# Gated cross-attention with two expert layers: the last stage's hidden layer computed transposed, its router weights spread over all partitions

## What is computed

```python
scores = jax.nn.sigmoid(x @ Wr)
_, idx = lax.top_k(scores + router_bias, TOP_K)              # 2 of 8 experts for each token
w = jnp.take_along_axis(scores, idx, axis=-1)
w = w / (jnp.sum(w, axis=-1, keepdims=True) + 1e-09)
cw = jnp.zeros((T, E), dtype=x.dtype).at[jnp.arange(T)[:, None], idx].add(w)
g = jnp.einsum('th,ehi->tei', x, Wg)                         # 4 networks, 256 -> 128
u = jnp.einsum('th,ehi->tei', x, Wu)
hid = jax.nn.silu(g) * u
mlp_out = jnp.einsum('tei,eih->teh', hid, Wd)                # 128 -> 256
routed = jnp.einsum('te,teh->th', cw[:, :E_MLP], mlp_out)
...
return routed + SHARED_SCALE * shared                        # shared: convolution over 4 tokens
```

## Time and profile before

| | before |
|---|---|
| median of 3 runs | 2226.85 us (2221.72 to 2227.82) |
| span of the profiled execution | 2225.1 us |
| PE busy | 2186.7 us, 98% |
| DVE busy | 1728.1 us, 78% |
| ACT busy | 1282.0 us, 58% |
| POOL busy | 645.1 us, 29% |
| last stage | from 1600.8 us to the end |

### The profile page before, as it was taken

One profiled execution on the slowest core, in us unless ns is written; L12 is line 12 of the kernel. 1 busy time (PEld: TensorE's weight loads), 2 busy tenths in 40 slices (PEclk: granted clock), 3 DMA queues, 4 the chain that ended last, 5 costly groups with the idle time before them and its releaser, 6 DMA issues. The chain is left out here.

```text
span 2225.1 us, 48355 instructions
## 1 busy us (share of the span) xinstructions
PE 2186.7 (98%) x15486; PEld 1865.5 (84%) x15486; DVE 1728.1 (78%) x6112; ACT 1282.0 (58%) x3251; POOL 645.1 (29%) x1162
## 2 busy tenths in 40 slices
PE   8999999999999999999999999999999999999997
PEld 6777777777777777777699999999878888888886
DVE  6788888888888888888675555555579999999986
ACT  6776776776776776776443333433345555555553
POOL 1123223222232232232220000000355555555541
PEclk9999999999999999999899999999999999999999
DMA  5320110110110110110052222221212222222210
GB/s 189 124 97 22 37 40 23 37 39 21 40 38 20 39 39 20 40 32 27 11 161 73 81 86 72 81 77 41 89 58 65 65 65 64 65 65 65 65 39 20
DMA packets 111642, 129.57 MB, mean 58 GB/s; under 512 B 14898, under 2 KB 98089, under 8 KB 111264
## 3 DMA queue, kind: packets, MB, share of 16 engines
q1 hardware_dynamic: 98249, 105.06, 14.9%
q0 software_dynamic: 12288, 21.21, 3.3%
q10 hardware_dynamic: 855, 0.19, 0.0%
HBM read 84.26 MB, written 54.53 MB: 62 GB/s over the span
## 5 line engine op out<-in xcount | busy, mean ns | idle before, releaser
L711 ACT ACTIVATE a_prob<-a_prob,a_nmax 128x376 f32<-128x376 f32 x512 | 309.7, 606 | 155.3 <-DVE a_nmax L857 155.3
L1457 ACT ACTIVATE e_hidden<-e_first,keep_b 128x256 f32<-128x256 f32 x320 | 134.1, 471 | 283.3 <-PE e_first L80 282.8
L857 DVE CUSTOM_DVE_ANT_0 a_prob<-a_score,a_mask_row 128x376 f32<-128x376 f32 x512 | 266.6, 540 | 10.8 <-issue 5.6
L80 PE MATMUL e_second<-e_w,e_hidden 128*128 128x256 f32 x1920 | 239.5, 284 | 0.0
L80 PEld LDWEIGHTS e_second<-e_w,e_hidden 128*128 128x128 f32 x1920 | 232.6, 192 | 0.0
L869 DVE TENSOR_SCALAR a_prob<-a_prob,a_rden 128x376 f32<-128x376 f32 x512 | 220.9, 453 | 2.5
L1151 PE MATMUL a_turned<-keep_ident,a_prob 128*128 128x128 f32 (+1 forms) x1536 | 217.3, 277 | 2.8 <-DVE a_probT L876 1.6
L1151 PEld LDWEIGHTS a_turned<-keep_ident,a_prob 128*128 128x128 f32 (+1 forms) x1536 | 173.5, 142 | 43.5 <-issue 27.6
L1142 PE MATMUL a_score<-a_kT,a_qT 64*128 64x376 f32 x1024 | 196.4, 502 | 0.0
L876 DVE COPY a_probT<-a_turned 128x384 f32<-128x384 f32 x256 | 139.8, 546 | 54.4 <-PE a_turned L1151 54.4
L719 ACT ACTIVATE a_probT<-a_turned 128x384 f32<-128x384 f32 x256 | 124.9, 488 | 92.1 <-PE a_turned L1151 91.7
(11 more groups left out here) (237 smaller groups left out, 5231.1 us busy)
## 6 DMA issues: line engine op xcount, KB each, us to landing
w_in<-W SPq DMA_DIRECT2D x32, 512.0 KB, 4.1
slots<-a_zeros SPq DMA_DIRECT2D x8, 1280.0 KB, 8.7
keep_rows<-slots SPq DMA_DIRECT2D x40, 256.0 KB, 3.9
answers<-e_y SPq DMA_DIRECT2D x40, 256.0 KB, 2.2
a_xn<-x SPq DMA_DIRECT2D x32, 256.0 KB, 2.9
a_xr<-x SPq DMA_DIRECT2D x32, 256.0 KB, 3.8
x<-r_x SPq DMA_DIRECT2D x32, 256.0 KB, 4.0
w_in<-x SPq DMA_DIRECT2D x32, 256.0 KB, 2.6
```

Of the source, the lines that this page charges most:

```text
L80: last = nc.tensor.matmul(out, stationary(a, t), moving(b, t), start=start and n == 0, stop=stop and n == len(todo) - 1)
L711: nc.scalar.activation(prob[:, u % 4, a], prob[:, u % 4, a], ACT.Exp, bias=nmax[:, u % 4, a:a + 1], scale=-1.0, accum_out=den[:, u % 4, a: ...
L857: nc.vector.tensor_tensor_reduce(prob[:, u % 4, a], score[SCORE_AT[u][a]][:, 0:NKV], mask_row[:, p], -1.0, 3.0e38, ALU.add, ALU.min, nmax[ ...
L1457: nc.scalar.activation(hidden[:, 2 * j + i], first[:, j, i * CH:(i + 1) * CH], ACT.Relu, bias=b1[:, 2 * j + i, bass.ds(e, 1)]).then_inc(re ...
```

## The change

- **Gate and up.** The weights of one network are now stationary and `x4T`, all 256 tokens of it, is moving: 12 matmuls of 256 columns for each pair `j` of networks, in place of 6 of 512 for each half of the tokens. The result has the hidden index on partitions and tokens along the row, for networks `2j` and `2j + 1`. `turn_hid` is gone.
- **Router weights.** A token's weight is now needed along the row, the same on all partitions. `cw` lies in a tile `cwp` padded to 32 columns. DVE transposes it in blocks of 32 (`weights_turned`), and SP writes the eight rows that matter, from each of the four blocks of partitions, to a DRAM tensor `chosen`, waits until they have landed, and reads all 4 KB of it back into every partition, into `cw_wide` (`spread_weights`).
- **The multiply** by these weights is done by POOL, on `hs`, in `share_hidden`, once for each pair. DVE then multiplies by `ups` in one instruction for each pair (`hidden`).
- **High and low parts** are made from `hid` in SBUF instead of from PSUM (`hidden_high` on ACT, `hidden_low` on DVE).
- **Down** sums by pairs of networks over both halves of the tokens, and both calls of `add_rest` are one. `down(s - 4, 0)` is at the end of PE's step now.

```diff
+            def spread_weights(b):
+                eng.wait_ge(cw_turned, b + 1)
+                for g in range(0, P, 32):
+                    eng.dma_start(t["chosen"][:, g:g + 32], cw_rows[g:g + EM * QT]).then_inc(cw_out, 16)
+                eng.wait_ge(cw_out, 16 * 4 * (b + 1))
+                at_least(eng, share_ok[1], b)
+                eng.dma_start(cw_wide[:].rearrange("p e s -> p (e s)"),
+                              t["chosen"].rearrange("c q -> (c q)").partition_broadcast(P)).then_inc(cw_in, 16)
...
             def step(s, p):
+                if live(s - 4):
+                    spread_weights(s - 4)
                 if live(s + 1):
                     early["load_x1"](eng, s + 1, 1 - p)
...
+            def share_hidden(b, j):
+                eng.wait_ge(hs_ok[j], b + 1)
+                eng.wait_ge(cw_in, 16 * (b + 1))
+                nc.gpsimd.tensor_tensor(hs[:, j].rearrange("p (e s) -> p e s", e=2),
+                                        hs[:, j].rearrange("p (e s) -> p e s", e=2), cw_wide[:, pair(j)],
+                                        ALU.mult).then_inc(share_ok[j], 1)
...
                 if live(s - 3):
                     norm4(s - 3)
+                if live(s - 4):
+                    share_hidden(s - 4, 0)
+                    share_hidden(s - 4, 1)
                 if live(s):
                     early["gather"](eng, s, p)
...
-            def weigh(b, p, i):
-                eng.wait_ge(hs_ok[i], b + 1)
-                eng.wait_ge(up_made[i], b + 1)
+            def weights_turned(b, p):
                 eng.wait_ge(route, N_ROUTE * (b + 1))
-                at_least(eng, hid_made[i], b)
-                for e in range(EM):
-                    es = slice(e * P, (e + 1) * P)
-                    nc.vector.scalar_tensor_tensor(hid[:, i, es], hs[:, i, es], cw[:, p, i, e:e + 1], ups[i][:, es],
-                                                   ALU.mult, ALU.mult).then_inc(hid_ok[i], 1)
+                at_least(eng, cw_out, 16 * 4 * b)
+                nc.vector.transpose(cw_rows[:], cwp[:, p]).then_inc(cw_turned, 1)
+            def hidden(b, j):
+                eng.wait_ge(share_ok[j], b + 1)
+                eng.wait_ge(up_made[j], b + 1)
+                at_least(eng, hid_low[j], b)
+                nc.vector.tensor_tensor(hid[:, j], hs[:, j], ups[j][:], ALU.mult).then_inc(hid_ok[j], 1)
...
-            def turn_hid(b, i):
-                eng.wait_ge(hid_ok[i], EM * (b + 1))
-                for e in range(EM):
-                    last = nc.tensor.transpose(gates[i][:, e * P:(e + 1) * P], hid[:, i, e * P:(e + 1) * P], ident[:])
-                last.then_inc(hid_made[i], 1)
...
-                split_product(nc, out[i][:].rearrange("p (e i) -> p e i", e=EM),
-                              lambda a, k: x4T[:, a, k, i * P:(i + 1) * P],
-                              lambda a, k: weight2(name, a, k), KD).then_inc(done[i], 1)
+                for e in range(2):
+                    last = split_product(nc, out[j][:, e * S:(e + 1) * S], lambda a, k: weight2(name, a, k)[:, 2 * j + e],
+                                         lambda a, k: x4T[:, a, k], KD)
+                last.then_inc(done[j], 1)
```

More of the change, by code:

```diff
@@ L2337, in step @@
                 if live(s - 4):
-                    weigh(s - 4, p, 1)
+                    hidden(s - 4, 1)
+                    hidden_low(s - 4, 0)
                 if live(s - 3):
@@ L2366, in down @@
                         eng.wait_ge(wd_low, 1)
-                split_product(nc, total[:, i * D:(i + 1) * D], lambda a, e: hidT[:, a, i, e],
-                              lambda a, e: wd2[:, a, e], EM, stop=False).then_inc(down_made[i], 1)
+                for i in range(QT):
+                    for n, (a, c, e) in enumerate((a, c, 2 * j + e) for e in range(2) for a, c in PASSES):
+                        last = nc.tensor.matmul(total[:, i * D:(i + 1) * D], hid2[:, a, e, i * P:(i + 1) * P],
+                                                wd2[:, c, e], start=j == 0 and i == 0 and n == 0, stop=False,
+                                                skip_group_check=True)
+                last.then_inc(down_made[j], 1)
             def values(b):
```

113 lines of the change are left out of this document (58 added, 55 removed).

## The result

| | before | after |
|---|---|---|
| median of 4 runs | 2227.25 us (2221.72 to 2227.82) | 2385.28 us (2383.44 to 2388.21) |
| ratio to before | | 1.0712 (95% interval 1.0696 to 1.0728) |
| span of the profiled execution | 2225.1 us | 2382.3 us |
| one step, mean of 28 | 18.6 us | 24.0 us |

The change makes the kernel 158 us slower, 7.1%; the forecast was 2396 us (2335 to 2470). A step here is the mean distance between the end T of the router chain that stands ahead of the first of the 28 steps (step 4) and the one that stands ahead of step 32. After the change these are 1632.73 and 2304.95, 28 steps of 24.0 us; before, 1633.58 and 2153.30, 18.56 us. From the second of them to the end of the last output it takes 74.0 us instead of 68.5.

What follows compares the result with a forecast made beforehand. PE bounds the old step at 18.48 us; writes, spread and two POOL multiplies ahead of the gather make a 24.4 us loop. 2226.85 + 28 steps x 5.9 (165) + 4 for the drain = 2396 us, range 2335 to 2470.

Steps and rivals of the forecast that it cites:

- DVE instructions with two SBUF sources only: Last-stage rival: POOL's multiplies meet DVE's convolution taps, each one of about 0.45 us; 25.3 us a step, 2421, inside the range.

Runs made afterwards that it cites:

- e13: e10 with `keep_x2` back at the head of POOL's step, so two instead of three large POOL instructions stand in a row; 2308.38 us.
- e10: Changed kernel, all computed, reordered: POOL does gather, first multiply, `keep_x2`, second multiply; hidden products moved on DVE and ACT, context on PE; 2390.40 us.
- e12: Kernel before the change, with two spare multiplies added on POOL behind `norm3`, at the end of its step; 2280.04 us.
- e1: Changed kernel with the gather put ahead of both multiplies on POOL, everything computed; 2373.58 us.

## What to carry to other kernels

When the profile shows one late link, ask for each of its neighbours when it would come if that link were gone: the second multiply needed a silu that comes 7.4 us after T, so that taking the spread away brought the copy forward by 0.95 us only, and to remove either the spread or the gather's wait gave less than 25 us. Before a large POOL instruction is added or moved, list what DVE runs at that time with its operands in SBUF: in e13 one POOL instruction moved so that two multiplies start 1.3 us later, behind the taps, and that was worth 3 us a step; and before an instruction is moved away, read which wait it covered at its old place. An engine at 90% can be a bound, when its idle time is latency in its own loop.

## What the hardware did that I had not expected

- A two-operand POOL instruction of 1.3 us holds a DVE instruction of 16 columns with one SBUF source: in 14 of the 28 steps `f_re` took 1.7 to 1.9 us instead of 0.17 and ended 0.04 to 0.05 us behind `f_x3p`. It had started 0.4 to 0.5 us ahead of `f_x3p`, beside the issue of the last gather. Memsets hold one of 256 columns, too (`f_x4h`, two in 1.46 us instead of 0.74). I had watched for DVE instructions with two SBUF sources only.
- When POOL instructions stand back to back, DVE isn't always let in between them: in e10 two taps took 4.94 us beside three of them, in e13 3.20 beside two; in e12 two DVE instructions took turns with two. Which of the two happens was not settled.
- One wait of PE of 2.00 us in e1 was followed by more than 6 us at the 1.2 GHz level.
- Four writes of 1 KB to DRAM were done 0.9 us after the issue of the last had ended, 2.17 us after that of the first began.
